# A two-layer perceiver on one core: maxima moved between tiles of the first layer, and unread products taken out of the second layer's opening

## The reference

```python
scores = jnp.einsum('bhqd,bhkd->bhqk', q * scale, k)
scores = scores + ((1.0 - attention_mask) * -10000.0)[:, None, :, :]
probs = jax.nn.softmax(scores, axis=-1)
ctx = jnp.einsum('bhqk,bhkd->bhqd', probs, v)
```

## Time and profile before

| | |
|---|---|
| median of 3 runs | 1073.76 us (1072.72 to 1075.67) |
| the profiled execution | 1068.03 us, its span 1066.3 us |
| PE busy | 1017.6 us, 95% of the span |
| DVE busy | 743.1 us, 70% |
| ACT busy | 679.0 us, 64% |
| POOL busy | 420.8 us, 39%, nearly all of it in the first layer |
| maxima of the second layer, DVE L756 | 339 of 620 ns |
| maxima of the first layer, DVE L753 | 396 of 621 ns |

### The profile page before, as it was taken

The page is one execution under the profiler, slowest core; times in us unless marked ns, Lnnn a source line. Parts: engine busy times, 40 slices in busy tenths (PEclk is TensorE's granted clock), DMA queues, the critical chain, the costliest instruction groups (busy, mean ns, idle before and its releaser), DMA issues. The chain is left out here.

```text
span 1066.3 us, 30777 instructions
## 1 busy us (share of the span) xinstructions
PE 1017.6 (95%) x12921; PEld 687.8 (65%) x12921; DVE 743.1 (70%) x1715; ACT 679.0 (64%) x953; POOL 420.8 (39%) x374
## 2 busy tenths in 40 slices
PE   8899999999999999998878899999999999999876
PEld 5466666676666666665544566667676666666665
DVE  4888888888888888876357666556665565566465
ACT  3677777777778777876542555566556666555722
POOL 4368888888888988881000000101100101000000
PEclk9999999999999999999998999999999999999999
DMA  8420122201221112112031010111100111000000
GB/s 313 140 71 20 54 70 71 67 23 53 71 72 34 45 65 70 53 66 93 10 120 68 2 36 2 37 36 37 36 8 30 37 37 36 2 2 2 2 1 5
DMA packets 14682, 53.31 MB, mean 50 GB/s; under 512 B 3025, under 2 KB 4817, under 8 KB 13649
## 3 DMA queue, kind: packets, MB, share of 16 engines
q1 hardware_dynamic: 14544, 51.35, 14.0%
HBM read 51.21 MB, written 0.13 MB: 48 GB/s over the span
## 5 line engine op out<-in xcount | busy, mean ns | idle before, releaser
L756 DVE TENSOR_REDUCE tile_max<-ps_max 128x1 f32<-128x448 f32 x339 | 200.7, 620 | 150.7 <-PE ps_max L1081 146.5
L753 DVE CUSTOM_DVE_ANT_0 unread<-ps_max,masks 128x448 bf16<-128x448 f32 x396 | 231.4, 621 | 67.4 <-PE ps_max L1081 66.2
L426 POOL TENSOR_TENSOR probs<-probs,masks 128x512 f32<-128x512 f32 x182 | 228.1, 1275 | 72.0 <-ACT probs L539 70.5
L551 ACT ACTIVATE probs<-ps_scores 128x1024 f32<-128x1024 f32 x193 | 187.2, 1021 | 86.2 <-PE ps_scores L1122 86.1
L546 ACT ACTIVATE probs<-probs 128x1024 f32<-128x1024 f32 x196 | 207.4, 1058 | 54.5 <-DVE probs L811 45.7
L1122 PE MATMUL ps_scores<-q_pad,k_full 32*128 32x256 f32 x3088 | 230.6, 377 | 0.0
L1139 PE MATMUL ps_out<-probs,values 128*32 128x128 f32 x6272 | 214.5, 277 | 0.7 <-ACT probs L551 0.4
L1139 PEld LDWEIGHTS ps_out<-probs,values 128*32 128x32 f32 x6272 | 159.4, 110 | 51.7 <-issue 48.0
L1122 PEld LDWEIGHTS ps_scores<-q_pad,k_full 32*128 32x128 f32 x3088 | 191.4, 186 | 0.7
L1081 PE MATMUL ps_max<-k_high,q_high 32*128 32x448 bf16 x735 | 180.1, 358 | 7.9 <-DVE tile_max L756 5.3
L1064 PE MATMUL ps_proj<-ctx_t,wk 128*128 128x448 f32 x384 | 168.8, 562 | 0.0
(11 more groups left out here) (258 smaller groups left out, 914.4 us busy)
## 6 DMA issues: line engine op xcount, KB each, us to landing
ctx_t<-in_ctx_t SPq DMA_DIRECT2D x28, 896.0 KB, 5.3
masks<-in_mask_n SPq DMA_DIRECT2D x14, 448.0 KB, 3.4
masks<-in_mask_t SPq DMA_DIRECT2D x14, 448.0 KB, 3.5
room_w<-in_L_attn_f_w SPq DMA_DIRECT2D x2, 1024.0 KB, 7.5
room_w<-in_L_ffn_w SPq DMA_DIRECT2D x2, 1024.0 KB, 8.8
room_w<-in_L_ffn_w_gate SPq DMA_DIRECT2D x1, 1024.0 KB, 10.6
room_w<-in_L_ffn_w_up SPq DMA_DIRECT2D x1, 1024.0 KB, 13.1
room_w<-in_L_ffn_w_down SPq DMA_DIRECT2D x1, 1024.0 KB, 15.0
```

Of the source, the lines that this page charges most:

```text
L426: nc.gpsimd.tensor_tensor(p, p, three(mask_t[m % 2], TILES)[:, t, :].unsqueeze(1).to_broadcast([P, 4, P]), ALU.add).then_inc(sig("bias_add ...
L551: nc.scalar.activation(prob(T, half), scores_half(T, half), ACT.Exp).then_inc(sig(f"exp_done{half}"), 1)
L753: ins = v.tensor_tensor_reduce(unread[:, j % 2, :], max_bank(m, j)[:, 0:HALF], mask_n[m % 2][:, HALF * half:HALF * (half + 1)], 1.0, -3e38 ...
L756: ins = v.tensor_reduce(tile_max[:, h, half:half + 1], max_bank(m, j)[:, 0:HALF], AX_X, ALU.max)
```

## The change

Three things are changed. The numbers of maxima behind the scores and behind the weighing: in the first layer tiles 5 and 6 get one behind the scores each, and tiles 0 and 2 lose the one behind the weighing. Those in tiles 5 and 6 go to the projections' bank, in block 0 (tile 6) too, and DVE reads them behind its masked add. At the opening of the second layer the unread product behind each pair of maxima is left out, and five instead of four stand ahead of the turn.

```diff
-        SCORED_AT = ((2, 0, 2, 1, 2, 0, 0), (2, 1, 2, 2, 2, 2, 2))
-        WEIGHED_AT = ((1, 2, 1, 2, 1, 2, 2), (0, 2, 1, 1, 0, 1, 0))
+        SCORED_AT = ((2, 0, 2, 1, 2, 1, 1), (2, 1, 2, 2, 2, 2, 2))
+        WEIGHED_AT = ((0, 2, 0, 2, 1, 2, 2), (0, 2, 1, 1, 0, 1, 0))
+
+        def late_bank(m, t):
+            return m < NB and t >= LAST_AT
+
+        def before_mask(m, t, count):
+            return 0 if late_bank(m, t) else count if m == 0 or m >= NB else min(count, 1)
...
-                            if m > 0 and k == 0 and len(here) == 2 and i == 0 and (t != SUMS_AT or m == NB):
+                            if k == 0 and (late_bank(m, t) or m > 0 and len(here) == 2 and i == 0 and (t != SUMS_AT or m == NB)):
                                 MAX_BANK[to, j] = 2
...
-                        early = behind_scores if l == 1 or m == 0 else behind_scores[0:1]
-                        for k, j in early:
+                        early = before_mask(m, t, len(behind_scores))
+                        for k, j in behind_scores[:early]:
                             maximum(k, j)
...
-                        for k, j in behind_scores[len(early):]:
+                        for k, j in behind_scores[early:]:
                             maximum(k, j)
...
                             beside_in(BESIDE_AT.index(i))
-                        elif i > 5:
-                            idle_products(1, ps_out)
...
-                idle_products(2 + 2 * l, ps_proj)
+                idle_products(2 + 3 * l, ps_proj)
                 turn_max(NB * l)
```

## The result

| | before | after |
|---|---|---|
| median | 1073.24 us (1067.93 to 1075.67, 6 runs) | 1062.2 us (1059.32 to 1063.51, 6 runs) |
| ratio | | 0.9905, 95% interval 0.9881 to 0.9929 |
| the profiled execution, its span | 1068.03, 1066.3 us | 1062.24, 1060.5 us |

The two profiled executions differ by 5.8 us, so half of the gain is not in the comparison of those two.

The account below looks back on a forecast made before the run. TensorE's instruction order was taken to bound a block (busy 33.50 of 33.73 us). First layer 6.2 us less, opening 0.3 more: -5.9, so 1067.8 us from a median of 1073.76; range 1063.5 to 1072.5, its own 1065.5 to 1069.5.

Parts of the forecast that it names:

- its twin in the second layer: Second layer's tile 0, same work in the new shape, 4.10 us; first layer's tile 0 should fall from 4.58 to that.
- the keys' wait: Tile 6: keys wait until DVE has read the added maximum in the projections' bank; 0.31 us lost, bounds 0.2 to 0.86.
- the forecast 6.2: First layer's sum in us saved: 0.52 in each of blocks 1 to 11, 0.83 in block 12, -0.31 in block 0.
- The cover by POOL and ACT: First layer: POOL's mask add falls 0.3 to 0.8 us late, but its result is weighed only next tile; no cost.
- POOL's narrow place: Tile 3: a POOL rounding ends at 258.95 and its mask add starts at 259.02.
- rival A: Tiles 2 and 3: POOL and ACT become the bound, the weighing waits; about half the gain lost, 1070.8 us; chance 0.16.
- Rival B: Tiles 5 and 6: DVE's chain, 0.55 later, delays turn and keys; 0.86 instead of 0.31, total 1074 us; chance 0.12.
- the half-clock end of the range: Second layer's opening: ten product matmuls take 4.3 us at half clock, the turn comes late; +0.8 us in sum.
- the +0.3 that I took: Second layer's opening: net loss of 0.3 us, the burst of products bringing the clock back partway; bounds -0.7 and +1.9.
- a sign that I had named: Sign of the forecast: first scores of the second layer within a us of where the sum puts them.
- rival C: Second layer's first block: half clock persists, four more tiles at 2.3 us each; 1078.7 us, slower than before; chance 0.06.
- the 5.7: Distance in us of the profiled execution, 1068.03, below the median 1073.76; carried over from summed 1062.1 to forecast 1067.8.

Follow-up runs that it names:

- the experiment with tile 6: The change with tile 6's added first-layer maximum put back behind the weighing of tile 2: tile 6 4.85 us, block 33.38; one execution 1060.37 us.
- fillings: More unread products in PE's lulls, such as blocks 0, 13 and 14; added to the whole change, against the kernel before: median 1058.91 us, ratio 0.988.
- the filled kernel: First layer's part of the change, products beside the maxima kept, more unread products in PE's lulls, against the kernel before: median 1057.95 us, ratio 0.9883.

## Why the prediction was wrong, point by point

**The first layer: right in its waits, each size within 0.15 us.** Tile 0 came to 4.10 as its twin in the second layer said. What I left out is the tile behind it: tile 1 went from 5.09 to 5.21. The 0.12 stand in its scores (from L1122 at 247.45 to the next work at 248.50, 1.05, before; from L1129 at 245.04 to 246.21, 1.17, after). The pair ahead, no longer held up at the end of tile 0, is issued right before them and is the likely cause; that was not tested. Tiles 0 and 1 together saved 0.36, tiles 2 and 3 0.38, where I had 0.48 and 0.40 for tiles 0 and 2. Tile 4 gave 0.06 that I did not have, tile 5 cost 0.02 for my 0.05, tile 6 0.34 for 0.31, and the keys' wait was 0.31 of it, as the experiment with tile 6 shows. The block lost 0.44 in place of 0.52; blocks 1 to 12 gave 5.65, block 0 took 0.34, together 5.3 for the forecast 6.2. Alone it measured 0.9937, 6.8 us, with an interval from 4.0 to 9.7.

**The cover by POOL and ACT: held.** POOL's narrow place went to no air at all in tiles 2 and 3, but no wait of PE for an exponential appeared, so rival A had the right place and no price. All that PE waited for from 74 to 445 us, the blocks 1 to 11, after the change (us in total, times, longest):
```profile
PE ps_scores L1163 <- DVE probs L818: 2.6, 11, 0.6
```
Rival B's chain ended 5.44 us into tile 5 for 5.41 before (268.78 and 271.49): its reads began 0.15 earlier in the tile and the second of its three steps took 0.31 in place of 0.67, which made room for the read that was added. In both traces that step ended 0.03 behind the end of one of POOL's adds (268.15 and 268.12 after, 270.87 and 270.84 before), in this block and in every other up to the twelfth within 0.05, so POOL seems to set its end; no run tests it.

**The opening up to the turn: the half-clock end of the range, not the +0.3 that I took.** I had -0.55 for the reductions and +0.8 in sum at half clock, and took +0.3 since the burst of products should bring the clock back partway; it did not, its ten matmuls took 4.43 us, and 4.3 was my figure for half clock. Without another lull in the way the maxima took 15.51 for 16.06 and the turn 4.50 for 3.15: +0.8. In the first profile after, an earlier fall at 551.7 added 1.6 to the maxima, so a sign that I had named failed: the first scores of the second layer came 2.8 us earlier than before (573.09 for 575.90), where the sum had 5.9.

**The step that failed: that everything behind the turn stays as it was.** My bounds for the opening were -0.7 and +1.9, I took +0.3, and in neither bound did I ask what becomes of the half clock in tiles 1 and 2 of block 14, though the rows with its price stood before me; I used them only for rival C, as a loss that might grow. They were a loss that could go. Block 14 went from 31.89 to 28.19, 3.7 us, in all four profiles of kernels without fillings that have no product beside the maxima and five ahead of the turn. The opening is thus worth +0.8 - 3.7 = -2.9 in these profiles against those of the kernel before; alone it measured 0.9974, 2.8 us (0.3 to 5.3). Against the profile of the first layer's part alone, which has the old opening and block 14 in 29.51, only 1.3 of the 3.7 are there. Filling tile 0 of the block, without any change to the opening, gave 3.6 in block 14 and 2.6 by the ratio. It is shown that what block 14 lost and got back is the clock; why the clock holds there behind a stretch at half clock is not. The stretch behind the turn has PE busy 1.66 of 3.00 us in both kernels (573.19 to 576.19 here, 576 to 579 before, each from 0.10 behind the first scores on). It is the row by which I judged a fall likely, and after the one the clock fell and after the other it did not.

**The baseline, the other step that failed.** I took the distance between the profiled execution of before and the median of three, 5.7 us, as a constant. The sum for the profiled execution was 1062.1 and the profile after came at 1062.24, by errors that cancel (0.9 more than forecast in the first layer, 1.4 less in the opening with block 14, 0.7 more at the end of the kernel, from half clock in lulls there). So by the prediction's own addition the whole miss, 1062.2 for 1067.8, came in with the 5.7. That distance is no constant: it is half clock in lulls, in some executions of before and not in others. Those of before at 1068 us have a mean granted clock of 0.991 to 0.992, those at 1073 0.987, those at 1075 to 1076 0.984; the kernel after has its profile at its own median, both at 0.989. By parts, 6.8 and 2.8 us by the ratios make 9.6, and the whole measured 10.2 and, repeated, 9.3. Against my 5.9, the opening with block 14 makes 3.1 of that, and the first layer, 6.8 for my 6.2, 0.6; its interval does not tell 6.8 from the 5.3 of its profile.

**Rival C** was not seen in the change, but exists: with three products ahead of the turn, and the fillings, the half clock did run into block 14 in the profiled execution, for tiles 0 and 1, and the block took 33.23 us for 28.32 with five.

**The rule that I weighed.** Without the products the clock fell among the maxima in all six profiles, at a price of 0.8 up to the turn. The Trainium skill ("TensorE: Matmul & The Clock Gate", section "What's actually happening") says that the slow clock is the resting state and that activity releases it. These six profiles agree; the one in which PE was busy for 17.00 of 17.00 us at a granted clock of 0.50 does not, and there the measurement decides. My inference, that removing unread products is never free, missed that the products themselves are dear once the clock is down: 2.01 us per pair for 1.00.

## What to carry to other kernels

Where an engine's order of work sets the time, a tile elsewhere in the same trace that already has the new shape is the best price, but price it with the tile behind it. Before forecasting an edit near a half-clock stretch, ask of each such stretch in the trace whether it stays, goes or grows, and put its whole price in the range with either sign. Compare profiled executions only after a look at how far single executions of the same kernel lie apart, and where; do not carry the distance between one profile and a median over to another kernel. The mean granted clock of each execution shows such distances without a profile.

## What the runs showed of the hardware that was not expected

Unread products beside work that is bound by another engine are not free at half clock: a pair of maxima with one product took 1.11 us at full clock (before) and 2.01 at half (the filled kernel), without product 1.00 at either (after). The clock stayed at 0.50 for 17 us of the filled kernel with PE never idle, in a mix of 128-row products and 32-row maxima, and came back at 577.3, during the unmixed products ahead of the turn (575.2 to 578.0). The same kernel, at the same 33.73 and 32.37 us per block, took between 1066.6 us, at a mean granted clock of 0.991, and 1079.7, at 0.981; in its three profiles the difference is which of its lulls were followed by half clock.
